# Last attention batch's back half between the first expert-weights batch's products; its closing sums over batches 1 to 4

## The reference

```
x = x + layernorm(attention(layernorm(x)))      # 16 heads, dots / ||dots||, no softmax
x = x + layernorm(soft_moe(layernorm(x)))       # 8 experts of 128 slots each

# soft_moe
xn = rmsnorm(x);  sn = rmsnorm(slot_embeds)
logits   = einsum('bnd,esd->bnes', xn, sn)
dispatch = softmax(logits over the 512 tokens n)
combine  = softmax(logits over all 1024 slots)
slots    = einsum('bnd,bnes->besd', xn, dispatch)
eo       = gelu(slots @ w1 + b1) @ w2 + b2
out      = einsum('bmd,bnm->bnd', eo, combine)
```

## Time and profile before

| what | value |
|---|---|
| median of 3 runs | 879.7 us (879.45 to 881.19) |
| the profiled execution's own time | 879.67 us |
| its span, first to last instruction | 877.9 us |
| PE busy | 842.2 us, 96% |
| DVE busy | 622.1 us, 71% |
| ACT busy | 538.4 us, 61% |
| POOL busy | 90.0 us, 10% |
| mean granted TensorE clock | 0.988 |

### The profile page before, as it was taken

How to read it: one execution, slowest core, us unless ns; L and a number is a source line. 1 busy time by engine, 2 the same in 40 slices (tenths; PEclk the granted TensorE clock), 3 DMA queues, 4 the chain that set the end, 5 groups by cost and what they waited for, 6 DMA issues and landing times. The chain is left out here.

```text
span 877.9 us, 16006 instructions
## 1 busy us (share of the span) xinstructions
PE 842.2 (96%) x5368; PEld 752.6 (86%) x5368; DVE 622.1 (71%) x1198; ACT 538.4 (61%) x1059; POOL 90.0 (10%) x97
## 2 busy tenths in 40 slices
PE   5899999879999999997999999999999999999998
PEld 4789998767888888886799999999999999999998
DVE  5788787758999989988575555565656564357886
ACT  4565565557876777776755555565546454467775
POOL 0100000013354233324000000000000000000000
PEclk9999999969999999999999999999999999999999
DMA  7011120113222222222402020202020205016883
GB/s 235 19 50 48 48 72 24 38 55 136 90 92 108 96 96 91 89 85 84 144 1 97 1 96 1 96 0 96 0 96 0 96 0 192 1 52 235 278 270 125
DMA packets 52266, 75.30 MB, mean 86 GB/s; under 512 B 3072, under 2 KB 33408, under 8 KB 52096
## 3 DMA queue, kind: packets, MB, share of 16 engines
q1 hardware_dynamic: 52224, 74.76, 24.9%
HBM read 49.59 MB, written 25.17 MB: 85 GB/s over the span
## 5 line engine op out<-in xcount | busy, mean ns | idle before, releaser
L854 PEld LDWEIGHTS bank<-w_r,act_r 128*128 128x128 f32 x1536 | 200.6, 191 | 12.7 <-DVE act_r L1683 2.6
L854 PE MATMUL bank<-w_r,act_r 128*128 128x256 f32 x1536 | 204.1, 283 | 1.6 <-DVE act_r L1683 1.6
L837 PE MATMUL bank<-sl_r,w_r 128*128 128x512 f32 x768 | 199.5, 395 | 3.6 <-DVE sl_r L1663 3.6
L1683 DVE TENSOR_TENSOR act_r<-act,act_r 128x512 fp32r<-128x512 f32 x128 | 88.6, 692 | 150.2 <-ACT act_r L1216 150.2
L1211 ACT ACTIVATE act<-bank,b_sb 128x512 f32<-128x512 f32 x128 | 88.0, 687 | 152.6 <-PE bank L837 151.9
L837 PEld LDWEIGHTS bank<-sl_r,w_r 128*128 128x128 f32 x768 | 137.3, 191 | 26.8 <-issue 3.9
L762 PE MATMUL bank<-disp_r,y_r 128*128 128x512 f32 x384 | 103.4, 406 | 1.0 <-DVE disp_r L1596 0.9
L737 PE MATMUL bank<-yT_r,snT 128*128 128x512 f32 x384 | 100.5, 398 | 0.0
L890 PE MATMUL bank<-eo_r,comb_r 128*128 128x258 f32 x768 | 92.5, 282 | 0.5 <-DVE eo_r L377 0.5
L890 PEld LDWEIGHTS bank<-eo_r,comb_r 128*128 128x128 f32 x768 | 92.2, 189 | 0.7 <-issue 0.7
L737 PEld LDWEIGHTS bank<-yT_r,snT 128*128 128x128 f32 x384 | 72.9, 191 | 15.8
(11 more groups left out here) (153 smaller groups left out, 1151.3 us busy)
## 6 DMA issues: line engine op xcount, KB each, us to landing
stage<-in_w SPq DMA_DIRECT2D x16, 1024.0 KB, 6.7
combine_scratch<-comb SPq DMA_DIRECT2D x64, 256.0 KB, 2.0
stage<-combine_scratch SPq DMA_DIRECT2D x4, 2048.0 KB, 9.3
snT<-combine_scratch SPq DMA_DIRECT2D x4, 2048.0 KB, 9.3
slots_eo<-in_x SPq DMA_DIRECT2D x8, 512.0 KB, 4.2
x_scratch<-stage SPq DMA_DIRECT2D x8, 512.0 KB, 3.0
x<-x_scratch SPq DMA_DIRECT2D x8, 512.0 KB, 3.9
x_d<-x_scratch SPq DMA_DIRECT2D x8, 512.0 KB, 9.5
```

Source lines behind the costliest of these rows:

```text
L837: last = pe.matmul(bank[i % RING][:, :], w1_r[q][:, a, k, j * P:(j + 1) * P], sl_r[f][:, c, k, :], start=(n == 0), stop=(n == len(steps) - 1))
L854: last = pe.matmul(bank[4 + 2 * f + c // 2][:, (c % 2) * D:(c % 2 + 1) * D], act_r[:, i % RING, a, c * S:(c + 1) * S], w2_r[q][:, w, j, :] ...
L1683: v.tensor_tensor(act_r[:, i % RING, 1, :], act[:, i % 2, :], act_r[:, i % RING, 0, :].bitcast(F32), ALU.subtract).then_inc(h_split, 1)
```

## The change

The back half of attention batch 7 and the first weights batch become one hand-written order, `last_back_and_first_weights`, on PE, ACT and DVE. Batch 0 has buffers of its own for logits and exponentials there: `neg_lt0` and `disp0` in parts of `slots_eo`, and small ones; they do not lie on the attention's memory. The scales and y of batch 0, and its transposes, are made in `attention(B - 1)`: `root_x2` and `scale_y` are now three calls, for batches 0 to 3, 4 to 6, and 7. The end of batch 7 is taken apart: `square_proj` and `root_proj` in weights batch 2, `add_proj` and `square_x2` in batch 3, `root_x2` and `scale_y` in batch 4. The scales of batches 4 to 6 are inverted in batch 1. As the projection of batch 7 stays in `stage` longer, the first expert's weights are loaded after batch 3's stores are issued, `sum_out_rows` goes to batch 5, `centre_out_rows` to batch 6. ACT's batches 2 to 6 and DVE's 2 to 4 are written out and no longer loops.

The diff, its core (SP, PE, ACT, DVE in this order):

```diff
             sp.wait_ge(x2_stored, 16 * (B - 4))
             load_x2(0)
-            with sp.Fori(B - 4, B) as b:
+            for b in (B - 4, B - 3):
                 store_x2(b)
+            sp.wait_ge(y_ready, 1)
+            load_x2(1)
+            store_x2(B - 2)
             attention_finished(sp)
-            sp.wait_ge(x2_squared, B * NT)
-            sp.wait_ge(x2_stored, 16 * B)
+            sp.wait_ge(x2_stored, 16 * (B - 1))
 
             def load_weights(e):
                 sp.dma_start(w1_raw, w1_v[:, ds(e * KD, KD), :]).then_inc(w_loaded, 16)
@@ -438,14 +467,20 @@
                 sp.dma_start(comb_v[:, ds(b * E + m, 1), :], comb[:, m % RING:m % RING + 1, :])\
                     .then_inc(comb_stored[m % RING], 16)
 
-            sp.wait_ge(y_ready, 1)
-            load_x2(1)
-            load_weights(0)
-            with sp.Fori(1, B - 1) as b:
+            def reload_and_store(b):
                 sp.wait_ge(y_ready, b + 1)
                 load_x2(b + 1)
                 for m in range(E):
                     store_combine(b - 1, m)
+
+            with sp.Fori(1, BH) as b:
+                reload_and_store(b)
+            store_x2(B - 1)
+            sp.wait_ge(x2_squared, B * NT)
+            sp.wait_ge(x2_stored, 16 * B)
+            load_weights(0)
+            with sp.Fori(BH, B - 1) as b:
+                reload_and_store(b)
             for b in (B - 2, B - 1):
                 for m in range(E):
```

```diff
-            def weights_of(b, u, first=False, second=False, last=False):
+            def last_back_and_first_weights():
+
+                b = B - 1
+                gram_times_q(b, False)
+                logits(0, 0, True)
+                outputs(b, False)
+                logits(0, 1, True)
+                norms(b)
+                logits(0, 2, True)
+                logits(0, 3, True)
+                transpose_o(b)
+                logits(0, 4, True)
+                transpose_dispatch(0, 0, True)
+                projection(b)
+                logits(0, 5, True)
+                transpose_dispatch(0, 1, True)
+                logits(0, 6, True)
+                transpose_dispatch(0, 2, True)
+                logits(0, 7, True)
+                transpose_dispatch(0, 3, True)
+                transpose_y(1, 1, True)
+                transpose_dispatch(0, 4, True)
+                fill_slots(0, 0, 0, 0, True)
+                transpose_dispatch(0, 5, True)
+                fill_slots(0, 0, 0, 1, True)
+
...
-            attention(B, front=False, first_y=True)
+                        fill_slots(b, 0, 0, m - 6)
+
+            attention(B - 1, before_y=True)
+            last_back_and_first_weights()
             attention_finished(pe)
-            weights_of(0, 0, first=True)
```

```diff
-            def weights_of(b, first=False, second=False, last=False):
+            def last_back_and_first_weights():
+
+                b = B - 1
+                square_proj(b - 1)
+                root_proj(b - 1)
+                square_x2(b - 1, 0, 3)
+                root_norm(b)
+                square_x2(b - 1, 3, 4)
+                root_x2(B // 2, B - 1)
+                exp_dispatch(0, 0, True)
+                exp_dispatch(0, 1, True)
+                round_oT(b, False)
+                for m in range(2, E):
+                    exp_dispatch(0, m, True)
+                    if m >= 3:
+                        round_dispatch(0, m - 3, True)
+                    if m == 5:
+                        round_y(0, 0, True)
+                    if m == 6:
+                        round_yT(1, first=True)
+                        round_y(0, 1, True)
+                round_dispatch(0, E - 3, True)
+
+            def weights_of(b, second=False, last=False):
                 for m in range(E):
-                    if second:
+                    if is_batch(b, 5):
                         if m:
                             sc.wait_ge(w2_summed, m)
                         sum_out_rows(m)
-                    if m % 2 == 0 and not first:
+                    if is_batch(b, 2) and m < NT:
+                        square_proj(B - 1, begin=m, end=m + 1)
+                    if is_batch(b, 2) and m == 5:
+                        root_proj(B - 1)
+                    if is_batch(b, 3) and m >= NT:
+                        square_x2(B - 1, m - NT, m - NT + 1)
+                    if is_batch(b, 4) and m == 3:
+                        root_x2(B - 1, B)
+                    if m % 2 == 0:
                         h, k = divmod(m // 2, KD)
                         keep_slots(b - 1, h, k)
-                    if first and m == 2:
-                        square_x2(B - 1, 0, NT)
                     if m in (4, 6):
-                        round_y(b, m // 2 - 2, first)
+                        round_y(b, m // 2 - 2)
                     if m == E - 1 and not last:
                         round_yT(b + 1)
-                    if m < 2 and not first:
+                    if m < 2:
                         round_dispatch(b - 1, E - 2 + m, second)
-                    exp_dispatch(b, m, first)
+                    exp_dispatch(b, m, False)
                     if m >= 2:
-                        round_dispatch(b, m - 2, first)
-                    if not first:
-                        exp_combine(b - 1, m)
-
```

```diff
+            def last_back_and_first_weights():
+
+                b = B - 1
+                keep_proj(b - 1, False)
+                times_q(b)
+                keep_logits(0, 0, True)
+                add_proj(b - 1)
+                keep_logits(0, 1, True)
+                clamp_norm(b)
+                scale_o(b)
+                keep_logits(0, 2, True)
+                invert_sum(0, 0)
+                keep_logits(0, 3, True)
+                invert_sum(0, 1)
+                rest_of_oT(b)
+                keep_logits(0, 4, True)
+                invert_sum(0, 2)
+                fold_min(0, 1, True)
+                rest_of_dispatch(0, 0)
+                invert_sum(0, 3)
+                keep_logits(0, 5, True)
+                keep_proj(b, False)
+                rest_of_dispatch(0, 1)
+                invert_sum(0, 4)
+                make_y(1, False)
+                keep_logits(0, 6, True)
+                rest_of_dispatch(0, 2)
+                invert_sum(0, 5)
+                keep_logits(0, 7, True)
+                fold_min(0, 2, True)
+                rest_of_dispatch(0, 3)
+                for k in range(KD):
+                    rest_of_yT(1, k)
+                invert_sum(0, 6)
+                fold_min(0, 3, True)
+                rest_of_dispatch(0, 4)
+                for m in (4, 5, 6):
+                    fold_min(0, m, True)
+                rest_of_dispatch(0, 5)
+                fold_min(0, 7, True)
+
...
+                    keep_logits(b, m, False)
                     if m:
...
-                    if m + 1 < E and not first:
+                    if m + 1 < E:
                         shift_combine(b - 1, m + 1, second)
+                    if second and m == 3:
+                        scale_y(1, B // 2, B - 1)
+                    if is_batch(b, 3) and m < NT:
+                        add_proj(B - 1, m, m + 1)
+                    if is_batch(b, 4) and m == 6:
+                        scale_y(2, B - 1, B)
                     if m:
-                        fold_min(b, m, first)
+                        fold_min(b, m, False)
                     if m >= 2:
                         rest_of_dispatch(b, m - 2)
                     if m == 5 and not last:
-                        make_y(b + 1, not first)
```

More of the change, by code:

```diff
@@ L1072, in attention, with round_yT, root_x2 @@
                     round_xn(b + 1)
+            def round_yT(b, first=False, at=6):
+                for k in range(KD):
+                    sc.wait_ge(yT_in_psum, b * KD + k + 1)
+                    if k == 0 and not first:
+                        sc.wait_ge(logits_in_psum, b * E)
+                    act_fn(yT_r[:, 0, k, :], bank[at + k][:, :], ACT.Copy).then_inc(yT_hi, 1)
+            def root_x2(begin, end):
+                sc.wait_ge(x2_squared, end * NT)
+                cols = slice(begin * NT, end * NT)
+                act_fn(roots[:, 0, cols], x2_sq[:, cols], ACT.Sqrt, bias=eps_ln[:], scale=1.0 / D)
+                act_fn(roots[:, 1, cols], x2_sq[:, cols], ACT.Sqrt, bias=zero_col[:], scale=1.0 / D)\
+                    .then_inc(y_rooted, 1)
             sc.wait_ge(consts_set, 1)
@@ L1085, in _ @@
                 attention(b)
[L1086 to L1100 removed]
+            attention(B - 1, following=False, before_y=True)
             def round_y(b, k, first=False):
@@ L1617, in weights_of @@
+            def weights_of(b, second=False, last=False):
+                invert_sum(b - 1, E - 1)
+                shift_of_tokens(b - 1, second)
+                rest_of_dispatch(b - 1, E - 2)
+                shift_combine(b - 1, 0, second)
                 for m in range(E):
-                    keep_logits(b, m, first)
-                    if first and m == 0:
```

(4 more changed lines are left out.)

221 lines of the change are left out of this document (115 added, 106 removed).

## The result

The changed kernel takes 872.85 us, median of 4 runs (872.09 to 875.09), against 879.58 of the kernel before in the same runs: ratio 0.9924, 95% interval 0.9907 to 0.9940. The forecast was 871.9: 6.7 us were gained where 7.8 were forecast. The profiled execution took 872.09 us with a span of 870.0.

What follows compares the result with a forecast made beforehand. TensorE, busy 96%, bounds the kernel, so only its waits and slowed clock at the attention-to-weights seam can give. 879.67 less 11.4 (seam) plus 3.6 (weights batches) gives 871.9 us; range 867.8 to 876.5.

Steps and rivals of the forecast that it cites:

- The walk: Seam, from batch 6's projection step by step to batch 1's second logits: there at 202.5 instead of 213.90, gaining 11.4 us.
- its list: Seam, DVE's operations from 186.0 up to the last fold: 13.6 us, setting `transpose_min` at 199.6.
- The clock rival: Seam: PE's waits fall close together and the clock falls again; 875.2 us, chance 13%.
- Table loads: Batch 2, ACT's load, root, load for `root_proj`: exponential 1.4 us late, PE waits 1.1 (bounds 0 and 2.8); no drain.
- Batch 4: ACT's load, two roots, load for `root_x2`: 3.05 less 1.26 idle and 0.3 slack, 1.5 us lost (bounds 0 and 3.1).
- the scales: Batch 4, `scale_y` in step 6 on DVE: 0.6 us lost (bounds 0 and 1.2).
- The weights' load: Batch 4: 2 MB ahead of the combine stores on SP; landing and need both at 14 us, covered by ACT's pause.
- signs of being wrong: Profile after: projection again 5 us, batch 2 and 4 waits missing or doubled, or DVE waiting for batch 4's combine store.
- the rival that the load makes the kernel slower: Batch 4: weights land late and DVE waits for the combine store; slower from 8 us late, 884 at 12; chance 3%.
- Batch 5: Batches 5 and 6 take over sums and centring from batches 1 and 2 at no cost: 0 us.
- Batches 1 and 3: DVE waits: 0.4 us for inverting scales in batch 1's fourth step, 0.5 for `add_proj` and a reciprocal in batch 3.
- The change is worth little: Whole kernel: half the seam's gain and losses at their upper bounds, put within 0.2%; chance 5%.

Runs made afterwards that it cites:

- e5: Changed kernel with three of DVE's running-minimum folds (steps 2, 3, 4) moved ahead of the sixth `keep_logits` in the seam; 871.50 us, seam 47.35.
- e4: Changed kernel with the seam's order on PE, ACT and DVE serial again: batch 7's back half, then batch 0's logits; 880.67 us, seam 56.40.
- e1: Changed kernel with batch 7's three square roots replaced by copies, so no table loads there (batch 7's result wrong); 872.62 us.
- e6: Changed kernel with early folds, split weights' load, batch 7's roots at starts of batches 3 and 4, scales at fourth step, squares and row sums at step ends; 867.68 us.
- e9: Against e6, batch 5's row sums and batch 2's squares one step later; one run, 866.09 us.
- e3: Changed kernel without batch 7's square roots and their table loads, and with the first expert's weights loaded in two halves; 870.38 us.
- e2: Changed kernel with the first expert's weights loaded in two halves, w1 one batch after w2; 872.50 us.
- e10: Against e6, DVE's batches 5 and 6 written out and not looped; one run, 866.19 us.
- e7: Changed kernel with batch 1's `scale_y` in the seventh step and not the fourth; one run, 874.99 us, batch 1 28.51.

## Why the prediction was right, and where it was off

**The seam.** The walk held step by step, and the forecast was right by its mechanism there. Forecast and measured, the latter 0.8 us early with the whole execution: norms issued by 175.2, `transpose_o` after two more logits at 177.20; projection of batch 7 at 181.6 and 181.13; PE's wait ahead of it 1.3 and 1.06; `transpose_min` 199.6 and 198.97; second logits of batch 1 202.5 and 201.66. DVE has no idle time from the sixth `keep_logits` at 185.65 to the end of the last fold, 13.2 us; its list was put at 13.6 from 186.0. The list was 0.4 us too long and its start, with the 0.8 taken into account, 0.4 too early, so that the end is right to 0.2 partly by luck. The six folds took 4.5, as forecast. e5 shows that this list was the right thing to add up: with three folds out it is 11.6 us long, 1.6 shorter, and the end moved by 1.6. e4 shows that the interleaving itself gives 7.4 of the 11.5, and the rest of the change the other 4.1. The forecast didn't say how the gain divides.

**The clock rival.** The pieces of wait, 1.06, 0.71, 0.64 and 1.46 us, did not bring the clock down. The granted clock is 1.00 throughout. After 4.14 us in e4 it was down again (0.50 from 176 to 183 us), as it was after 2.63 before (0.50 from 179 to 182).

**Table loads.** Four new switches in batches 2 and 4 (the pair between batches 0 and 1 is gone), and no gap behind any of them: 243.37 + 1.28 to 244.66, 244.98 + 1.28 to 246.27, 294.00 + 1.28 to 295.29, 295.80 + 1.28 to 297.09. The drain that the Trainium skill, "ScalarE: Activation LUTs", What ACT_TABLE_LOAD costs, adds to each switch appears nowhere. e1 gives a pair a price of 1.42 us in batch 2, where 1.1 was forecast from ACT's idle time. The step was right and short by 0.3. Against e1, counted from the second logits of the batch, the exponential came 1.82 us later, where the walk had 1.4: the combine exponential ahead of the pair began 0.26 us later in the batch than in the kernel before (13.59 us behind those logits, 13.33 before), and from its start to the exponential it took 3.64 us and not 3.4. Of the 1.82 the slack behind it took up 0.4, where the forecast had 0.3. The squares also cost 0.28 by themselves (27.66 in e6, 27.38 in e9), where I had put nothing.

**Batch 4.** Forecast 1.5 for the pair and 0.6 for the scales; measured 2.94. e3 gives the pair with its cover 1.8. The scales cost 1.1, where I took 0.6: the term was priced by batch 1's five operations of the kernel before, at a place where POOL was idle; here one of them waited for POOL. Pair and scales together make batch 4 the largest miss, 0.8 us. The forecast's own picture of the profile, a pause of PE of about 1.5 us behind `root_x2`, did not appear as one: PE waited 0.86 and 1.16 us, the second behind the scales.

**The weights' load.** The forecast had the store landing at about the time that it was needed, covered by ACT's pause. It was needed 13.2 us into the batch (294.8, logits of batch 4 from 281.64) and landed at 15.8, 2 later than forecast. The cover held (e1, e2, e3), so the error cost nothing in the sum. DVE's wait for a combine store in batch 4 was one of the forecast's signs of being wrong, and it came, with 2.67 us. What failed is the statement that store and need meet at 14 us; that ACT's pause covers the wait held, and the rival that the load makes the kernel slower did not come true.

**Batch 5** was put at nothing and cost 0.63. That batches 1 and 2 did the same sums "without a wait for them" was true (27.33 in batch 1 before), and it did not carry over: the row sum ahead of the rounding (e9) and DVE's late first keep, which written-out code removes (e10), fell together in the first steps of batch 5.

**Batches 1 and 3** cost 0.04 and 0.34, where 0.4 and 0.5 were forecast. These two terms were too large and hide a part of the others' shortfall.

**The sum.** -11.4 + 3.6 against -11.5 + 5.0: 1.4 us missed on the losses, 1.0 us in the median. Against the terms that were too small (0.6 in batch 2, 0.8 in batch 4, 0.6 in batch 5) stand 0.5 us from those that were too large.

**A rival that was added up wrongly.** "The change is worth little" took half of the seam's gain, 5.7 us, with all losses at their upper bounds. These bounds add up to 9.6 us, so this case would be 3.9 us slower than before and not within 0.2%. Its 5% belong to the slower side; the measured time touches neither.

## What to carry to other kernels

When the end of one stage and the beginning of the next wait on different engines, weave them by hand and add up the list of each in-order engine between two marks; the longest list gives the end. Put the work pushed out of the seam where an engine demonstrably waits (a batch's first step), not where it merely has a lower busy share: the same table pair cost 1.42 us in the sixth step of batch 2 and about nothing in the first step of batch 3 (27.70 against 27.64). And test two stalls that end together as a pair, since either one taken away alone showed nothing here (0.06 us each, 1.80 together).

## What the runs showed of the hardware

A tensor_scalar of 4 or 12 columns on DVE took 1.18 to 1.24 us instead of 0.17 where POOL's 128x512 subtraction had begun just before it (batch 1 in e7; batch 4 in the changed kernel, in e1 to e5 and in e7), and in the two places shown it ended 0.03 us after it. DVE's first `keep_logits` behind the entry of a loop stood 0.57 us behind the instruction ahead of it, 0.23 written out; in the kernel before another such entry showed 0.22, so the cause stays open. Two stalls of 2.67 us (DVE, for a DMA) and 3.1 us (ACT, table loads and roots) that ended 0.4 us apart cost 1.80 us together and, each taken away alone, gave 0.06. A combine store issued behind a 2 MB load on the same queue landed 8.3 us after its issue, where the median of such stores is 2.0. Executions of kernels that are alike up to there reach the same instruction at 150.0 to 151.6 us.
